# First rows split ahead of the value weights, K and Q ahead of the values, and the output weights' pieces behind the first two pairs' maxima

## What is computed

```python
x = x + attn(layernorm(x))             # the part that the change touches
x = x + cross_attn(layernorm(x), ctx)  # 64 context rows
x = x + ffn(layernorm(x))              # 256 -> 1024 -> 1024 -> 1024 -> 256

def attn(x):                           # H = 16, head size 64
    q, k, v = x @ w_q, x @ w_k, x @ w_v
    a = softmax(causal(q @ k.T / 8))   # rows t, columns s <= t
    return (a @ v) @ w_o
```

## Time and profile before

| what | value |
|---|---|
| median of three runs | 1500.75 us (1499.98 to 1501.02) |
| the profiled execution, its own time | 1502.59 us |
| its span in the trace | 1500.8 us |
| TensorE matmuls (PE) busy | 1482.6 us, 99% |
| VectorE (DVE) busy | 1150.4 us, 77% |
| ScalarE (ACT) busy | 970.7 us, 65% |
| GpSimd (POOL) busy | 490.5 us, 33% |

### The profile page before, as it was taken

The page is one execution under the profiler, slowest core; times in us unless marked ns, Lnnn a source line. Parts: engine busy times, 40 slices in busy tenths (PEclk is TensorE's granted clock), DMA queues, the critical chain, the costliest instruction groups (busy, mean ns, idle before and its releaser), DMA issues.

```text
span 1500.8 us, 29190 instructions
## 1 busy us (share of the span) xinstructions
PE 1482.6 (99%) x10584; PEld 1253.7 (84%) x10584; DVE 1150.4 (77%) x2892; ACT 970.7 (65%) x2274; POOL 490.5 (33%) x763
## 2 busy tenths in 40 slices
PE   8999999999999999999998999999999999999999
...
GB/s 155 2 2 2 30 2 29 2 2 30 1 29 2 2 30 2 2 30 1 22 64 81 177 104 91 131 124 105 90 99 95 206 113 85 85 85 85 86 85 43
DMA packets 60633, 90.30 MB, mean 60 GB/s; under 512 B 5952, under 2 KB 38080, under 8 KB 60480
## 3 DMA queue, kind: packets, MB, share of 16 engines
...
...
## 4 chain that ended last, share of the span: by engine, by line
PE 85%; DVE 5%; issue 4%; SPq 2%; ACT 2%; DMA 1%; POOL 0%; DVEq 0%; POOLq 0%
PE bank L1050 14%; PE bank L1052 12%; PE bank L666 10%; PE bank L586 9%; PE bank L638 8%; PE bank L588 8%; PE bank L587 7%; PE bank L650 6%; PE bank L1209 2%; PE bank L1200 2%; SPq L1686 2%; PE bank L1058 2%; PE bank L1176 1%; PE bank L1167 1%; PE bank L1165 1%
## 5 line engine op out<-in xcount | busy, mean ns | idle before, releaser
L852 POOL TENSOR_SCALAR P<-P,stats 128x512 f32<-128x512 f32 (+3 forms) x512 | 268.7, 543 | 378.4 <-DVE stats L830 378.2
L725 ACT ACTIVATE P<-P,stats 128x384 f32<-128x384 f32 (+3 forms) x512 | 283.9, 560 | 16.4 <-DVE stats L822 16.2
L689 ACT ACTIVATE PT<-bank 128x512 fp32r<-128x512 f32 (+1 forms) x384 | 185.4, 525 | 87.5 <-PE bank L650 86.5
L822 DVE CUSTOM_DVE_ANT_0 P<-bank,cmask 128x384 f32<-128x384 f32 (+3 forms) x512 | 228.5, 483 | 1.1 <-PE bank L638 0.9
L739 DVE TENSOR_TENSOR PT<-bank,PT 128x512 fp32r<-128x512 f32 (+1 forms) x384 | 219.0, 595 | 5.2 <-ACT PT L689 4.1
L1371 DVE TENSOR_TENSOR Hb<-gt,Hb 128x512 fp32r<-128x512 f32 x128 | 90.8, 710 | 167.1 <-ACT Hb L1217 165.5
L1050 PE MATMUL bank<-Hb,hw 128*128 128x512 f32 x512 | 201.3, 393 | 0.8 <-DVE Hb L1371 0.8
L1050 PE MATMUL bank<-w,hw 128*128 128x512 f32 x512 | 199.2, 389 | 0.0
L666 PEld LDWEIGHTS bank<-PT,V 128*128 128x128 f32 x1024 | 165.5, 191 | 22.2 <-DVE PT L739 4.3
L666 PE MATMUL bank<-PT,V 128*128 128x512 f32 (+3 forms) x1024 | 177.3, 321 | 3.5 <-DVE PT L739 3.5
L1052 PE MATMUL bank<-Hb,hw 128*128 128x512 f32 x448 | 174.8, 390 | 0.0
...
## 6 DMA issues: line engine op xcount, KB each, us to landing
...
xs<-x_scratch SPq DMA_DIRECT2D x23, 512.0 KB, 4.2
...
stageA<-in_h SPq DMA_DIRECT2D x14, 512.0 KB, 3.8
x_scratch<-x SPq DMA_DIRECT2D x8, 512.0 KB, 3.0
x_scratch<-xs SPq DMA_DIRECT2D x8, 512.0 KB, 2.9
...
```

The source lines that it names most:

```text
L689: return e.activation(dst, src, ACT.Copy, scale=scale)
L725: e.activation(p, p, ACT.Exp, bias=st_[:, k:k + 1], scale=-1.0, accum_out=st_[:, 8 + k:9 + k]).then_inc(s_exp, 1)
L822: e.tensor_tensor_reduce(P_tile(P, i, a), banks["S", P, max(i, 1)][a][:, slice(*S_COLS[i])], cmask[:, 512 - n:512], -1.0, 3.0e38, ALU.add, ...
L852: e.tensor_scalar(p, p, stats[P % 4][:, k:k + 1], 1.0, ALU.mult, ALU.mult).then_inc(s_norm, 1)
```

## The change

- On ACT and DVE the first rows' parts stand ahead of piece 2 (value weights). The parts of K and Q of pair 0 go between pieces 4 and 6, those of the first values behind piece 6.
- On TensorE `k.0 q.0` stand ahead of `v.0`, and `idle.1` is 36 transposes where it was 60.
- `project` waits for each half of the rows by itself, and for the low half only ahead of the matmul that reads it.
- Pieces 8 and 9 move back on both engines: piece 8's low part from ahead of the maxima of pair 0 to behind four maxima of pair 1, piece 9's from behind `r.0.2` to ahead of `r.1.2`.
- Batch 1's layer norm moves back: `ls.1 lc.1` from among the maxima of pairs 0 and 1 to ahead of those of pair 2, `ln0.1 ln2.1` to behind them, `rs.1` on POOL to behind `yl.0`.

```diff
     "PE": """
-        idle.0 rows.0.0 rows.0.1 idle.1 v.0 k.0 q.0 k.1 v.1 v.2 S.0.3 S.0.2 S.0.1 q.1 v.3 S.1.3 S.1.2 k.2 T.0.2
+        idle.0 rows.0.0 rows.0.1 idle.1 k.0 q.0 v.0 k.1 v.1 v.2 S.0.3 S.0.2 S.0.1 q.1 v.3 S.1.3 S.1.2 k.2 T.0.2
...
     "ACT": """
-        wh.0 wh.1 wh.2 rows_high.0.0 rows_high.0.1 wh.3 wh.4 wh.5 wh.6 vh.0 kh.0 qh.0 wh.7 kh.1 vh.1 wh.8 vh.2
+        wh.0 wh.1 rows_high.0.0 rows_high.0.1 wh.2 wh.3 wh.4 kh.0 wh.5 qh.0 wh.6 vh.0 wh.7 kh.1 vh.1 vh.2
...
     "DVE": """
-        ls0a ls.0 lc.0 wl.0 ln0.0 ln2.0 wl.1 wl.2 rows_low.0.0 rows_low.0.1 wl.3 wl.4 wl.5 vl.0 wl.6 kl.0 ql.0
+        ls0a ls.0 lc.0 wl.0 ln0.0 ln2.0 wl.1 rows_low.0.0 rows_low.0.1 wl.2 wl.3 wl.4 kl.0 wl.5 ql.0 wl.6 vl.0
...
     "POOL": """
-        con con2 rs.0 n.0.3.1 n.0.2.1 n.0.3.0 n.0.2.0 n.0.0.0 n.0.0.1 rs.1 n.0.1.1 n.0.1.0 n.1.3.1 n.1.2.0
+        con con2 rs.0 n.0.3.1 n.0.2.1 n.0.3.0 n.0.2.0 n.0.0.0 n.0.0.1 n.0.1.1 n.0.1.0 n.1.3.1 n.1.2.0 n.1.2.1
...
@@ idle_work
-            for n in range((20, 30)[k]):
+            for n in range((20, 18)[k]):
...
@@ project
-            w.wait_ge(s_xlo, xT_done(b))
+
             for c in range(2):
-                m = mm3(out[:, :], W[:, 0, c, fs], W[:, 1, c, fs], X[:, 0, c, :], X[:, 1, c, :], c == 0, c == 1)
+                w.wait_ge(s_xhi, xT_done(b) - 1 + c)
+                e.matmul(out[:, :], W[:, 0, c, fs], X[:, 0, c, :], start=c == 0, stop=False)
+                e.matmul(out[:, :], W[:, 1, c, fs], X[:, 0, c, :], start=False, stop=False)
+                w.wait_ge(s_xlo, xT_done(b) - 1 + c)
+                m = e.matmul(out[:, :], W[:, 0, c, fs], X[:, 1, c, :], start=False, stop=c == 1)
             m.then_inc(s_qk, 1)
```

More of the change, by code:

```diff
@@ L41 @@
[L41 to L43 removed]
+        wh.0 wh.1 rows_high.0.0 rows_high.0.1 wh.2 wh.3 wh.4 kh.0 wh.5 qh.0 wh.6 vh.0 wh.7 kh.1 vh.1 vh.2
+        e.0.2.1 e.0.2.0 e.0.1.0 qh.1 e.0.3.1 e.0.3.0 e.0.0.1 e.0.1.1 vh.3 e.0.0.0 wh.8 e.1.3.0 ph.0.2.1 ph.0.2.0
@@ new lines @@
+        e.1.2.0 kh.2 e.1.3.1 wh.9 vh.4 e.1.2.1 ph.0.0.1 ph.0.1.1 ph.0.0.0 e.1.1.0 ph.0.1.0 qh.2 kh.3 e.1.0.1
+        yo.0.0 e.1.0.0 e.1.1.1 yo.0.1 ph.1.2.0 ph.1.2.1 e.2.3.0 qh.3 e.2.3.1 ph.1.1.0 e.2.2.0 ph.1.0.0 ph.1.0.1
+        e.2.0.0 kh.4 ph.1.1.1 e.2.0.1 qh.4 e.2.2.1 e.2.1.1 e.2.1.0 vh.5 e.3.3.1 e.3.2.0 yo.1.0 e.3.3.0 yo.1.1
+        ph.2.0.1 ph.2.0.0 e.3.2.1 ph.2.2.1 vh.6 ph.2.2.0 vh.7 ph.2.1.1 ph.2.1.0 e.3.0.1 e.3.0.0 yo.2.0 e.3.1.0
+        e.3.1.1 e.4.3.0 yo.2.1 e.4.3.1 ph.3.2.1 ph.3.2.0 ph.3.0.0 ph.3.0.1 e.4.2.0 ph.3.1.1 e.4.2.1 ph.3.1.0
@@ L44 @@
+        e.4.1.1 e.4.0.1 e.4.0.0 kh.5 qh.5 e.4.1.0 yo.3.0 yo.3.1 ph.4.2.0 ph.4.2.1 e.5.2.1 ph.4.0.1 ph.4.0.0 kh.6
         rows_high.1.0 e.5.3.0 ph.4.1.0 ph.4.1.1 e.5.2.0 e.5.1.1 rows_high.1.1 e.5.3.1 qh.6""",
     "DVE": """
-        ls0a ls.0 lc.0 wl.0 ln0.0 ln2.0 wl.1 wl.2 rows_low.0.0 rows_low.0.1 wl.3 wl.4 wl.5 vl.0 wl.6 kl.0 ql.0
-        wl.7 kl.1 vl.1 wl.8 m.0.2.1 m.0.2.0 m.0.1.0 m.0.3.1 m.0.0.1 m.0.3.0 vl.2 ql.1 m.0.1.1 m.0.0.0 r.0.2 wl.9
-        ls.1 m.1.3.0 m.1.2.0 r.0.0 lc.1 vl.3 pl.0.2.0 m.1.3.1 m.1.2.1 kl.2 pl.0.2.1 ln0.1 vl.4 m.1.1.0 pl.0.0.1
@@ L49 @@
-        pl.0.1.1 pl.0.0.0 pl.0.1.0 ql.2 r.1.2 m.1.0.1 kl.3 m.1.0.0 m.1.1.1 ln2.1 ys.0.0 r.1.0 ys.0.1 m.2.3.0
-        pl.1.2.0 pl.1.2.1 m.2.3.1 m.2.2.0 m.2.2.1 ql.3 m.2.1.1 m.2.0.0 m.2.1.0 m.2.0.1 pl.1.1.0 pl.1.0.1
-        pl.1.0.0 kl.4 pl.1.1.1 ql.4 r.2.2 m.3.3.1 vl.5 m.3.2.0 r.2.0 m.3.3.0 m.3.2.1 ys.1.0 ys.1.1 pl.2.0.1
+        ls0a ls.0 lc.0 wl.0 ln0.0 ln2.0 wl.1 rows_low.0.0 rows_low.0.1 wl.2 wl.3 wl.4 kl.0 wl.5 ql.0 wl.6 vl.0
+        wl.7 kl.1 vl.1 vl.2 m.0.2.1 m.0.2.0 m.0.1.0 m.0.3.1 m.0.0.1 m.0.3.0 ql.1 m.0.1.1 m.0.0.0 r.0.2 m.1.3.0
@@ L52 @@
+        m.1.2.0 r.0.0 vl.3 pl.0.2.0 m.1.3.1 m.1.2.1 wl.8 kl.2 pl.0.2.1 vl.4 m.1.1.0 pl.0.0.1 pl.0.1.1 pl.0.0.0
+        pl.0.1.0 ql.2 wl.9 r.1.2 m.1.0.1 kl.3 m.1.0.0 m.1.1.1 ys.0.0 r.1.0 ys.0.1 ls.1 lc.1 m.2.3.0 pl.1.2.0
+        pl.1.2.1 m.2.3.1 m.2.2.0 m.2.2.1 ql.3 m.2.1.1 m.2.0.0 m.2.1.0 m.2.0.1 ln0.1 pl.1.1.0 pl.1.0.1 pl.1.0.0
+        kl.4 ln2.1 pl.1.1.1 ql.4 r.2.2 m.3.3.1 vl.5 m.3.2.0 r.2.0 m.3.3.0 m.3.2.1 ys.1.0 ys.1.1 pl.2.0.1
         pl.2.0.0 r.3.2 pl.2.2.1 vl.6 pl.2.2.0 vl.7 pl.2.1.1 m.3.0.1 m.3.0.0 pl.2.1.0 m.3.1.0 m.3.1.1 m.4.3.0
```

10 lines of the change are left out of this document (3 added, 7 removed).

## The result

| | before | changed |
|---|---|---|
| median of 20 runs each | 1500.28 us (1497.11 to 1502.85) | 1502.44 us (1500.16 to 1505.25) |
| the profiled execution, its own time | 1502.59 us | 1502.72 us |
| its span | 1500.8 us | 1500.9 us |

The ratio is 1.0013, with an interval of 1.0007 to 1.0019. The changed kernel is 2.0 us slower (1.1 to 2.8), where the forecast was 0.8 us faster. That is within the 0.2% that were called no change, but the sign is the other one, the interval leaves out 1, and the median is outside the forecast range. A second measurement gave 1.0013 again.

The account below looks back on a forecast made before the run. The prediction took PE's own work as the bound behind the head and DVE as the gate at `S.3.3` within it. A gain of 0.8 us took the profiled 1502.59 to 1501.8, or 1499.95 on the median, range 1497.8 to 1501.6.

Parts of the forecast that it names:

- The low clock goes as well, worth 1.6 us: First projections, 13.85 to about 17.4 us: with no gap ahead, some eight matmuls run at full clock, worth 1.6 us.
- ledger: Check by DVE's totals up to `S.3.3`: 38.0 us busy plus 3.9 idle, ending at 53.1, a gain of 0.3 us.
- The sum is the same with or without this, because DVE decides: Head up to `S.3.3`: the forecast sum does not depend on PE keeping full clock in the first projections.
- steps 1 and 2: DVE from 11.28 us through the first projections' parts: maxima of pair 0 start at 21.1, `r.0.2` at 25.3, 4.5 us earlier.
- Step 3: POOL's first four normalisings take 2.64 us (other bound 3.38); `T.0.2` starts at 28.0, `pl.0.2.0` at 29.35, 5.4 us earlier.
- Step 4: The change's cost: DVE stands idle for 1.65 us in front of `pl.0.2.0`, where `wl.9`, sums and scale stood.
- Step 5: DVE from `pl.0.2.0` to the maxima of pair 2: 14.1 us instead of 10.85, reaching 43.5, 2.1 us earlier.
- Step 6: DVE from the maxima of pair 2 to the end of `pl.1.1.1`: 9.0 us; `S.3.3` at 52.5, 0.9 us earlier.
- Walk: Sum of DVE's single steps through the head: `S.3.3` at 52.5, a gain of 0.9 us; 0.8 was taken.
- DVE as the gate: At `S.3.3`, PE waits for DVE's `pl.1.1.1` and can pass no more than about 0.3 us earlier unless DVE does.
- The rival in which PE keeps its early start: `S.3.3` up to 4.7 us earlier, 1496.0 us; chance 0.08 for a gain above 3, 0.12 for 1.8 to 3.
- The rival "slower": Clock falls two or three times behind PE's waits from 41 to 53 us, median slower by 2.4 to 4.0; chance 0.03.

Follow-up runs that it names:

- b3: The kernel before, unchanged, traced once more, on another chip than its first repeats; this execution took 1500.27 us.
- b4: The kernel before, unchanged, one further trace; this execution took 1499.52 us.
- e5: The changed kernel with `wl.8` moved into DVE's idle time ahead of `pl.0.2.0`; 1502.7 against 1499.47 us for the kernel before, ratio 1.0017.
- a2: The changed kernel, unchanged, traced again; this execution took 1500.71 us.
- e1: The changed kernel with 14 filler transposes on PE ahead of `T.1.1`; 1502.45 against 1500.74 us for the kernel before, ratio 1.0008.
- a3: The changed kernel, unchanged, traced and timed again; traced execution 1501.29 us, timing 1502.01 against 1500.12 us for the kernel before, ratio 1.0013.
- a4: The changed kernel, unchanged, one further trace; this execution took 1500.38 us.
- e4: The changed kernel with the old start, pieces 8 and 9 and the norm still late; 1505.9 against 1500.74 us for the kernel before, ratio 1.0036.
- e6: The changed kernel with `ls.1 lc.1` behind `ql.3` instead of ahead of `m.2.3.0`; 1501.31 against 1499.47 us for the kernel before, ratio 1.0012.
- e8: The kernel before with the new start and the late norm, pieces 8 and 9 in their old place; 1503.3 against 1499.47 us, ratio 1.0027.
- e2: The changed kernel with the whole norm further back, among pairs 3 and 4; 1500.92 against 1500.74 us for the kernel before, ratio 1.0004.
- e3: The kernel before with the new start alone, pieces and norm in their old place; 1498.74 against 1500.74 us, ratio 0.9991.

## Why the prediction was wrong

**The baseline.** The sum was made against the profiled execution and carried over to the median as a constant 1.84 us. That is the step that failed most. The profiled execution came to `S.3.3` at 53.35, 1.8 and 2.3 us later than b3 and b4, of which 1.4 to 1.6 are the fall of the clock at 14 us; its long fall near 811 us cost it another 0.7 against theirs. The median execution, as far as its time and clock tell, is of the kind of b3 and b4. "The low clock goes as well, worth 1.6 us" counted as a gain of PE's what most executions of before, by that inference, didn't lose. With `S.3.3` at 51.3 as the reference, the prediction's own ledger (53.1) says 1.8 us slower, and 2.0 was measured; that this is so close is partly luck, as the ten traces give 1.6 in the head and nothing over the whole execution.

**"The sum is the same with or without this, because DVE decides"** is the reasoning that hid it, and it was wrong. In b3 and b4, with no change but a full clock at 14 us, DVE's own last step `pl.1.1.1` starts at 50.7 and 50.2 and not at 52.5. Part of the 2.7 us in which DVE stood idle before was waiting for what the slow projections wrote: from 10 to 54 us it waits 0.9, 0.7 and 0.3 us for parts of V, Q and K in the profiled execution, and in b3 only 0.5, for Q. So the margin of 0.3 us between DVE and PE at `S.3.3` did not mean that DVE could come no earlier.

**The start (steps 1 and 2)** was right: `k.0` at 10.41 (forecast 10.7), full clock, scores of pair 0 at 18.79, 5.0 us earlier (up to 4.7), first maximum of pair 0 at 20.62 (21.1), `r.0.2` at 25.00 (25.3).

**Step 3** was right: POOL's first four took 2.51 us, nearest to the 2.64 taken, and `T.0.2` started at 27.84 (28.0). The other bound, 3.38, was the duration with `wl.9` beside it; in e5, with `wl.8` beside them, all eight of pair 0 took 5.08 us instead of 4.12.

**Step 4** was right: DVE idle for 1.60 us (1.65), `pl.0.2.0` at 29.04 (29.35).

**Step 5** was 1.0 us too small: from `pl.0.2.0` to `m.2.3.0` 15.12 us instead of 14.1. Of that, 0.56 is the scale, which took 0.75 us behind POOL's subtraction, where before it takes 0.19. The waits for ACT (0.26 and 0.37) were 0.1 above the 0.5 allowed, and the rest, 0.3, is in the pitches. So the gap ahead of `T.1.1` became 1.80 us, above my largest of 1.6.

**Step 6** was right in its length: 8.8 us from `m.2.3.0` to the end of `pl.1.1.1` in a2 (9.0).

**Walk or ledger.** They gave 52.5 and 53.1, and the walk was taken because it goes by single steps. Without a fall the changed kernel shows 53.34 to 53.66, and e1 53.15: the ledger was the nearer one. Its busy time of DVE was 38.0 and is 37.67. The walk came out early because it left waits out.

**DVE as the gate** was right for the kernels with the late norm where the clock held: PE waits 1.2 to 1.4 us for `pl.1.1.1` in a2, a3, a4, e1, e4, e5, e6 and e8. In the two traces with the fall PE came later than DVE let it. The 7 us of waits that PE was to have were 5.2. The rival in which PE keeps its early start came only in e2 and e3, which have the norm elsewhere.

**The rival "slower"** had the right mechanism, the clock behind PE's gaps between 41 and 53 us, and got 0.03. It happened in two of five traces, behind 1.80 us and not near 2.3, and cost 1.5 us once. Averaged over the five traces that is 0.6 of the 1.6 us, the smaller part. The larger part was no rival at all: that the kernel before can be, and probably mostly is, quicker through its head than its profile.

**"Behind `S.3.3` nothing differs"** holds for the order, and up to 718 us for the offset. It does not hold for the spans: near 811 us the profiled execution of before had the long fall and that of the changed kernel had none, which hides the 1.35 us of the head in the two spans.

**Left open.** The median difference of 2.0 agrees with the heads of five traces each (1.6) and with the timed executions at equal mean clock (1.5), and no more than that. In the traces the fall near 811 us is rarer with the changed kernel (1 of 5 against 5 of 5); the mean clocks of the timed executions, lower with the change, speak against that being the rule, and where they lost it was not settled. Not tried: the change with only the norm in its old place, which the experiments point to, with the pieces late and `ls.1 lc.1` between the maxima of pairs 0 and 1. Of the kernels run, none beats the kernel before by more than 0.2%.
